# A cross-attention and expert layer: all tokens through sorted expert blocks in two phases, none through all experts

## The reference

```python
# x: (8, 256, 256); ctx: (8, 120, 256); 16 heads; 8 experts; all float32
x = x + xattn(layernorm(x), ctx, ctx, Wq, bq, Wk, bk, Wv, bv, Wo, bo, mask, key_mask)
hs = layernorm(x).reshape(-1, 256)                  # 2048 tokens
probs = softmax(hs @ router_w + router_b)           # 8 experts
idx = argmax(probs); gate = probs[idx]
expert_out = einsum('th,ehd->ted', hs, expert_w) + expert_b
x = x + (one_hot(idx) * gate) combined with expert_out   # one expert per token
```

## Time and profile before

| what | value |
|---|---|
| median of three runs | 257.46 us (257.45 to 258.82) |
| the profiled execution's own time | 259.96 us |
| its span, first to last instruction | 258.2 us |
| mean granted clock of PE | 0.921 of 2.4 GHz |
| busy: PE, DVE, ACT, POOL | 221.6, 156.4, 117.1, 74.6 us |
| chain that ended last | PE 54%, DVE 23%, ACT 6%, issue 6%, DMA 5%, POOL 4% |

### The profile page before, as it was taken

How to read it: one execution, slowest core, us unless ns; L and a number is a source line. 1 busy time by engine, 2 the same in 40 slices (tenths; PEclk the granted TensorE clock), 3 DMA queues, 4 the chain that set the end, 5 groups by cost and what they waited for, 6 DMA issues and landing times.

```text
span 258.2 us, 5042 instructions
## 1 busy us (share of the span) xinstructions
PE 221.6 (86%) x1696; PEld 153.1 (59%) x1696; DVE 156.4 (61%) x499; ACT 117.1 (45%) x254; POOL 74.6 (29%) x100
## 2 busy tenths in 40 slices
PE   7599988898988989989998995853969969999994
PEld 2376556476656666566675553532767757776683
DVE  4358763756787878779648563482433545565564
ACT  0646664665745754863763555416322340531000
POOL 6155762051144054035004004030113044124400
PEclk9979997999999999999999999995555989999799
DMA  6894005000001001000001001014121113211001
GB/s 212 305 365 137 1 1 163 7 3 1 3 0 44 1 3 41 4 0 22 23 3 41 0 3 41 4 43 116 53 62 49 55 41 94 74 50 54 20 20 41
DMA packets 12164, 14.19 MB, mean 55 GB/s; under 512 B 2257, under 2 KB 10729, under 8 KB 12138
## 3 DMA queue, kind: packets, MB, share of 16 engines
q1 hardware_dynamic: 9932, 8.79, 11.3%
q0 software_dynamic: 1488, 3.18, 3.5%
q10 hardware_dynamic: 720, 1.91, 2.2%
HBM read 9.09 MB, written 5.69 MB: 57 GB/s over the span
## 4 chain that ended last, share of the span: by engine, by line
PE 54%; DVE 23%; ACT 6%; issue 6%; DMA 5%; POOL 4%; SPq 1%; ACTq 0%; DVEq 0%; POOLq 0%
PE ps L426 11%; DVE nm L1086 10%; PE ps L414 7%; PE ps L496 5%; PE ps L492 4%; PE ps L613 4%; PE ps L420 4%; ACT pr L769 3%; DMA kp<-in_key_mask_dram 3%; PE ps L466 3%; PE ps L611 3%; PE ps L520 2%; PE ps L597 2%; PE ps L507 2%; PE ps L614 2%
## 5 line engine op out<-in xcount | busy, mean ns | idle before, releaser
L769 ACT ACTIVATE pr<-ps 120x512 f32<-120x512 f32 x64 | 33.0, 602 | 16.5 <-PE ps L496 16.5
L1086 DVE TENSOR_REDUCE nm<-ps 128x4 bf16<-128x480 f32 x64 | 37.5, 648 | 3.2 <-PE ps L470 3.2
L346 POOL DMA_INDIRECT out_dram<-e_nat,hb x19 | 18.8, 988 | 51.4 <-DVE e_nat L1133 49.4
L341 POOL DMA_INDIRECT rows_by_expert<-xr,slot x12 | 12.2, 1019 | 50.2 <-DVE slot L1055 48.3
L775 ACT ACTIVATE ou<-ps 128x512 f32<-128x512 f32 x16 | 9.6, 597 | 26.5 <-PE ps L507 24.3
L492 PE MATMUL ps<-tT,sel 128*120 128x512 bf16 x64 | 18.5, 403 | 1.8 <-ACT tT L820 1.4
L1141 DVE SCALAR_TENSOR_TENSOR xr<-ps,dsp,xr 128x256 f32<-128x256 f32 x32 | 15.5, 483 | 6.5 <-PE ps L414 5.8
L426 PE MATMUL ps<-xT,w_nat 128*128 128x256 f32 x64 | 16.6, 404 | 2.9 <-ACT xT L792 2.9
L322 POOL TENSOR_TENSOR rs<-ve,mhalf 128x2 f32<-128x2 f32 x8 | 5.6, 701 | 46.2 <-DVE ve L964 46.2
L507 PE MATMUL ps<-pr,va 120*32 120x256 f32 x256 | 17.5, 386 | 0.7 <-ACT pr L769 0.6
L597 PE MATMUL ps<-identf,hnb 128*128 128x128 f32 x38 | 9.6, 343 | 9.7 <-ACT hnb L755 7.6
(11 more groups left out here) (151 smaller groups left out, 510.4 us busy)
## 6 DMA issues: line engine op xcount, KB each, us to landing
hb<-rows_by_expert SPq DMA_DIRECT2D x19, 130.0 KB, 2.1
xr<-in_x_dram SPq DMA_DIRECT2D x8, 256.0 KB, 7.3
e_nat<-in_expert_w_dram SPq DMA_DIRECT2D x2, 1024.0 KB, 7.4
rows_by_expert<-zer SPq DMA_DIRECT2D x1, 1040.0 KB, 11.1
ctxs<-in_ctx_dram ACTq DMA_DIRECT2D x1, 840.0 KB, 6.9
out_dram<-xr SPq DMA_DIRECT2D x4, 128.0 KB, 1.7
out_dram<-e_nat,hb POOLq DMA_INDIRECT x19, 2.4
w_nat<-in_Wk_dram ACTq DMA_DIRECT2D x1, 256.0 KB, 3.4
```

The costliest lines, as they stand in the source:

```text
L346: pool.indirect_dma_start(out_rows, bass.IndirectOffsetOnAxis(ap=hb[:, j % HR, C_ID:C_ID + 1].bitcast(U32), axis=0), ob[:, j % HR, :], Non ...
L769: act.activation(pr[:, r, :, :], SC[r][0:S, :], ACT.Exp, scale=SCALE).then_inc(s("a_exp"), 1)
L1086: v.tensor_reduce(nm[:, b % 2, h, :, 2 * r:2 * r + 2], SC[r][:, 0:G * S].rearrange("p (c e s) -> p c e s", c=KC, e=2), AX_X, ALU.max, nega ...
```

## The change

All eight batches are sorted. Phase 0 holds batches 0 to 4 (10 tiles, 17 blocks), phase 1 batches 5 to 7 (6 tiles, 13 blocks), each with HBM rows, zeros, counts and a block table of its own; 30 blocks in all. `dense_unit`, its sums and its bias product are gone. The table of phase 0 is worked out at the beginning of `i` = 7, and the loads follow; the pipeline ends with `i` = 7. What was left of batches 6 and 7 is written out by hand between block steps 0 to 10; steps 11 and later are blocks alone.

The rows carry the normalised values besides the plain ones (`CW` = 514 words), so ACT no longer normalises a block, and PE transposes from the loaded buffer. The scale and offset stay in SBUF (`rs2`, `nb2`). `oner` and `ebp` have 128 rows, of which two are used and the rest are zero. PE looks up the expert's number inside the block step instead of at set places ahead. `block_low` and `block_out` are the two halves of DVE's former `block_part`.

```diff
-    SB = B - 2
-    NS = SB * TH
-    NB = NS + E - 1
+    FB = (0, 5, B)
+    NSP = [(FB[p + 1] - FB[p]) * TH for p in range(2)]
+    NBP = [n + E - 1 for n in NSP]
...
-    CW = D + 4
-    C_RS, C_NB, C_GATE, C_ID = D, D + 1, D + 2, D + 3
+    CW = 2 * D + 2
+    C_HN, C_GATE, C_ID = D, 2 * D, 2 * D + 1
...
-        ebp = sb("ebp", [33, E, D], F32R)
-        oner = sb("oner", [33, P], F32R)
+        ebp = sb("ebp", [P, E, D], F32R)
+        oner = sb("oner", [P, P], F32R)
...
-            sp.dma_start(rows_d.rearrange("(e r) d -> r e d", e=E)[0:P],
-                         zer[:, :].unsqueeze(1).to_broadcast([P, E, CW])).then_inc(s("d_z"), 16)
+            zeros = zer[:, :].unsqueeze(1).to_broadcast([P, E, CW])
+            sp.dma_start(rows_d[0].rearrange("(e r) d -> r e d", e=E)[0:P], zeros).then_inc(s("d_z0"), 16)
...
+            sp.dma_start(rows_d[1].rearrange("(e r) d -> r e d", e=E)[0:P], zeros).then_inc(s("d_z1"), 16)
...
-            sp.wait_ge(s("v_be"), 2)
-            sp.wait_ge(s("d_z"), 16)
-            sp.wait_ge(s("d_sc"), 16 * NS)
-            for j in range(NB):
-                load_block(j)
-            for t in range(NS, NT):
-                sp.wait_ge(s("v_dn"), (t // TH - SB) * NU + (EP - 1) * TH + t % TH + 1)
-                sp.dma_start(out[t // TH, (t % TH) * P:(t % TH + 1) * P, :], xr[:, t, 0:D]).then_inc(s("d_out"), 16)
+            for p in range(2):
+                sp.wait_ge(s("v_be"), 2 * p + 1)
+                sp.wait_ge(s(f"d_z{p}"), 16)
+                sp.wait_ge(s(f"d_sc{p}"), 16 * NSP[p])
+                for j in range(NBP[p]):
+                    load_block(NBP[0] * p + j)
...
-                pool.memset(oner[:, :].bitcast(F32), 1.0).then_inc(n, 1)
+                pool.memset(oner[:, :].bitcast(F32), 0.0).then_inc(n, 1)
                 pool.memset(ebp[:, :, :].bitcast(F32), 0.0).then_inc(n, 1)
-                pool.wait_ge(n, NLATE - 2)
+                pool.wait_ge(n, NLATE - 3)
+                pool.memset(oner[0:2, :].bitcast(F32), 1.0).then_inc(n, 1)
...
-                if i == B:
-                    for j in range(EARLY):
-                        store_block(j)
-                if 0 <= i - 2 < SB:
+                if 0 <= i - 2:
                     scatter(i - 2)
                 if 0 <= C < B:
                     rsqrt2(C)
-            for j in range(EARLY, NB):
+            store_block(0)
+            store_block(1)
+            rsqrt2(B - 1)
+            for j in range(2, 6):
                 store_block(j)
-
-
-
-        STEPS = {B: [[], [0], [1], [2], [3, 4], [5], [6, 7], [8]],
-                 B + 1: [[9, 10], [11], [12], [13], [14, 15], [16], [17, 18], [19, 20]]}
-        DENSE = {B: [[], [], [], [], [], [], [], [0]],
-                 B + 1: [[], [1], [2], [3], [4], [5], [6], [7]]}
-        SUMS = {B + 1: [[0], [], [1], [2], [3], [4], [5], [6]]}
-
-
-        LOADS = {B: [[], [0, 1], [2], [3, 4], [5], [6], [7, 8], [9, 10]],
-                 B + 1: [[11], [12, 13], [14], [15, 16], [17], [18], [], []]}
-
-        def at(table, i, f):
-            return table[i][f] if i in table else []
-
-        def left(table, n):
-            return range(max(sum(table[B + 1], [])) + 1, n)
+            scatter(B - 2)
+            for j in range(6, 9):
+                store_block(j)
+            scatter(B - 1)
+            for j in range(9, NB):
...
-            def load_experts(js):
-                for j in js:
-                    if j == 0:
-                        pe.wait_ge(s("v_be"), 1)
-                    if j < NB:
-                        experts[j] = pe.value_load(be[0:1, j:j + 1], min_val=0, max_val=E - 1)
 
             def block_step(j):
                 if j < NB:
-                    pe.wait_ge(s("a_hb"), j + 1)
+                    if j in (0, NBP[0]):
+                        pe.wait_ge(s("v_be"), 2 * phase_of_block(j) + 2)
+                    experts[j] = pe.value_load(be[0:1, j:j + 1], min_val=0, max_val=E - 1)
+                    pe.wait_ge(s(f"d_hb{j % HR}"), 16 * (j // HR + 1))
                     if j == 0:
                         pe.wait_ge(s("v_mx"), 2 * NP * B)
+                        pe.wait_ge(s("a_exp"), 2 * NP * B)
                     if j >= 2:
                         pe.wait_ge(s("v_bL"), j - 1)
                     for k in range(KC):
-                        t = pe.transpose(TURN[j % 2][:, k * P:(k + 1) * P], hnb[:, j % 2, k * P:(k + 1) * P], identf[:, :])
+                        t = pe.transpose(TURN[j % 2][:, k * P:(k + 1) * P],
+                                         hb[:, j % HR, C_HN + k * P:C_HN + (k + 1) * P], identf[:, :])
...
-            def dense_unit(u):
...
-                        if R == SB - 1:
-                            c_hidden_turn(R)
-                        elif isC:
...
+            c_out_turn(B - 1)
+            block_step(0)
+            block_step(1)
+            c_norm_turn(B - 1)
+            block_step(2)
+            c_project(B - 1)
+            block_step(3)
+            c_hidden_turn(B - 2)
+            block_step(4)
+            c_logits(B - 2)
+            block_step(5)
+            block_step(6)
+            pe.wait_ge(s("a_hT"), B - 1)
+            c_hidden_turn(B - 1)
+            r_ranks(B - 2)
+            block_step(7)
+            c_logits(B - 1)
+            block_step(8)
+            block_step(9)
+            block_step(10)
+            r_ranks(B - 1)
+            for j in range(11, NB + 2):
...
-                    act.activation(hnb[:, j % 2, :], hb[:, j % HR, 0:D], ACT.Identity, scale=hb[:, j % HR, C_RS:C_RS + 1],
-                                   bias=hb[:, j % HR, C_NB:C_NB + 1]).then_inc(s("a_hb"), 1)
...
+                    a = act.activation(xr[:, t, C_HN:C_HN + D], xr[:, t, 0:D], ACT.Identity, scale=rs2[:, t:t + 1],
+                                       bias=nb2[:, t:t + 1])
...
+            block_high(0)
+            block_high(1)
+            norm_high(B - 1)
+            hidden(B - 2)
+            block_high(2)
+            block_high(3)
+            hidden_high(B - 2)
+            block_high(4)
+            hidden(B - 1)
+            block_high(5)
+            gate_exp(B - 2)
+            block_high(6)
+            hidden_high(B - 1)
+            block_high(7)
+            block_high(8)
+            gate_exp(B - 1)
+            for j in range(9, NB):
+                block_high(j)
...
+            def block_step(j):
+                if j < NB:
+                    block_low(j)
+                if j >= 2:
+                    block_out(j - 2)
...
+                        if i == B - 1:
+                            blocks(0)
...
+            hidden_offset(B - 2)
+            normalise(B - 1)
+            block_step(0)
+            block_step(1)
+            block_step(2)
+            residual(B - 1)
+            block_step(3)
+            block_step(4)
+            hidden_offset(B - 1)
+            route_logits(B - 2)
+            block_step(5)
+            route_choice(B - 2)
+            block_step(6)
+            slots(B - 2)
+            block_step(7)
+            route_logits(B - 1)
+            block_step(8)
+            route_choice(B - 1)
+            block_step(9)
+            block_step(10)
+            slots(B - 1)
+            blocks(1)
+            for j in range(11, NB + 2):
+                block_step(j)
```

More of the change, by code:

```diff
@@ L194, in xattn_moe_kernel, with phase, phase_of_block, place_in_cum @@
         block = es.enter_context(nc.Block())
-        ITER = range(-1, B + 2)
-        UB = [(OV, PJ)[n % 2] for n in range(NU)] + [(OV, PJ, TR)[n % 3] for n in range(NU)]
-        def unit(u):
-            b, n = SB + u // NU, u % NU
-            return b, n // TH, n % TH, UB[u]
+        ITER = range(-1, B)
+        def phase(b):
+            return int(b >= FB[1])
+        def phase_of_block(j):
+            return int(j >= NBP[0])
+        def place_in_cum(t):
+            return t + phase(t // TH)
         TURN = [SC[0][:, 0:D], SC[1][:, 0:D]]
@@ new lines, in block_low, with block_out @@
+            def block_low(m):
+                v.wait_ge(s("a_bH"), m + 1)
+                if m >= 3:
+                    v.wait_ge(s("p_by"), m - 2)
+                v.tensor_tensor(bL[:, m % 3, :, :], TURN[m % 2].rearrange("p (k t) -> p k t", k=KC),
+                                bH[:, m % 3, :, :].bitcast(F32), ALU.subtract).then_inc(s("v_bL"), 1)
+            def block_out(m):
+                v.wait_ge(s("p_by"), m + 1)
+                if m >= HR:
+                    v.wait_ge(s(f"d_o{m % HR}"), 16 * (m // HR))
+                v.scalar_tensor_tensor(out=ob[:, m % HR, :], in0=PROD[m % 2], scalar=hb[:, m % HR, C_GATE:C_GATE + 1],
+                                       in1=hb[:, m % HR, 0:D], op0=ALU.mult, op1=ALU.add).then_inc(s("v_by"), 1)
```

300 lines of the change are left out of this document (82 added, 218 removed).

## The result

The changed kernel took 246.75 us (median of 4 runs, 243.45 to 248.84), the kernel before 257.45 beside it; the ratio is 0.950, interval 0.939 to 0.962. The direction was forecast, the size was not: 232 was said, with a range to 243, so the gain is 10.7 us where 25.5 were expected. The profiled run took 246.34, its span 244.5 at a mean granted clock of 0.944.

The account below looks back on a forecast made before the run. It took PE's tail to be bound by gaps, low clock and inefficient blocks; the new tail, laid out through 175.9, 198.5, 208.0, 212.3 and 229.7, gave span 232.3, 25.9 less, so 232 us, range 227 to 243.

Parts of the forecast that it names:

- The bias product on 128 rows: Expert block step on PE: 1.15 us at full clock instead of 1.44, about 2.0 instead of 2.52 at low clock.
- the check by parts: Whole kernel: 23 us of dense units less 13 for new blocks, 5.5 from cheaper old blocks, some 10 from gaps and clock.
- Rival (a): Block step: the gap of the bias product stays, 1.44 us a block; time 236, chance 0.08.
- Up to ranks(7): Last attention stage and block steps 2 to 10: batch 7's norm turn at 175.9 us, ranks(7) at 198.5, partly low clock.
- (c): Tail from 176 us: the clock stays low to the end, steps at 2.0; time 246, chance 0.09.
- (d): Tail: slower than before, clock low and blocks at the old low-clock price of 2.52; time 264, chance 0.03.
- the second lands 2.9 after its issue at 201.3, at 204.3: Phase change: landing of batch 7's last scatter, which leads to block 17 being there at 208.0 us.
- the ring of eight buffers, ... 10.3 for eight, 1.29: Last 13 blocks: store landing, SP, load, three steps and output take 10.3 us per eight blocks, 1.29 each.
- The 1.45: Last 13 blocks: us taken per block, expecting queueing above the competing rates; twelve intervals give 17.4.
- Rival (b): Block step limited elsewhere, by the lookup inside it or 257 KB loads taking 4.2 us; time 242, chance 0.09.
- landing 2.4 and the closing waits 0.2: Kernel end: us from the last store at 229.7 to the span's end at 232.3.
- Rival (e): Whole change: the parts cancel and little comes; chance 0.02.

Follow-up runs that it names:

- c2: The kernel before with only the bias product changed, read from 128 rows instead of 33; 248.91 us, ratio 0.966.
- e4: The changed kernel with the bias product back on 33 rows; 253.84 us, ratio 0.978 to the kernel before.
- g1: d3 with the expert lookups of all blocks put back; 235.99 us, ratio 0.912.
- g3: d3 without the constant products that hold the clock; 237.59 us, ratio 0.918.
- g5: g1 with each lookup a load alone, without the arithmetic and bounds test behind it; 235.4 us, ratio 0.910.
- d3: The changed kernel with one expert lookup, 258-word rows of plain values, twelve load buffers and constant products in PE's waits; 234.52 us, ratio 0.905.
- g2: d3 with rows of 514 words and the normalised values again; 237.23 us, ratio 0.911.
- d2: The changed kernel with the last four stores written directly by SP to a spare buffer; 240.66 us, ratio 0.932.
- c3: The changed kernel with constant, unused products in PE's waits to hold the clock; 245.26 us, ratio 0.949.
- c1: The changed kernel run again unchanged, as control; 249.41 us, ratio 0.967.
- d1: The changed kernel run again unchanged, as control for another set; 246.26 us.

## Why the prediction was right in direction and wrong in size

*The bias product on 128 rows*: right, and its gain on the low side. 1.15 was taken, 1.09 and 1.05 measured, and the part alone brought 9.7 us (c2) where the check by parts gave it 5.5 and a share of the gaps. It is followed after 0.21 and not the 0.12 said. Rival (a) is out. The Trainium skill ("TensorE: Matmul & The Clock Gate", "Why this matters for your kernels") has a product over 32 rows take what one over 128 takes. No run has 32 rows; with 33 these traces do not agree, 0.32 behind the product in e4 against 0.21 on 128 rows in the kernel after. Its other rule (same page, "LDWEIGHTS (loading the stationary operand)"), that the weight load does not depend on the rows, does agree: 0.18 and 0.19. What differs is that around the 33-row product the loads did not run ahead of their products.

*Up to ranks(7)*: right, 1.4 late at the norm turn and 1.4 at the ranks. The clock fell at 166 and again at 190, as far as "part of it low" says. One reading behind it was loose: the block work at the low level before the change was not "without a gap", PE being busy for only 1.04 us of those from 190 to 193. Two slips in the working touch only rivals (c) and (d): the 10.3 of project, turns and logits at the low clock stands on no row, and (d) decides from a step of 2.29, not 2.26.

*The phase change*: **the first step that failed, and by size the largest, is "the second lands 2.9 after its issue at 201.3, at 204.3"**. It was issued at 204.08, 2.8 late (1.4 of it since the ranks), and landed in 5.1, at 209.2. The 2.9 had been scaled from a landing with little other traffic, where here the DMA engines moved 245 GB/s (206 to 209); with half rows the same scatter landed in 2.5 in three runs of four (g1, g3, g5; 4.3 in d3). Then came a wait that the forecast did not have, 1.2 for the landing of block 9's store: the buffers of the second phase are those of the first, and I let the ring begin only behind block 17. SP and the load took 3.4 of their 3.6. Behind that, block 17's store came 6.4 after its transposes and not 4.3: 1.3 of it is the low clock of its first steps, the rest is spent at POOL, where block 16's store went 1.29 ahead of it.

*The last 13 blocks*: **the second step that failed is "the ring of eight buffers, ... 10.3 for eight, 1.29"**, worth 1.8 us here. The ring turns in six blocks, not eight, since PE does the products of block j − 2 behind the transposes of block j. With my own durations that gives 2.4 + 1.04 + 2.6 + 1.15 + 0.8 = 8.0 for six, 1.33, so most of the rest is landings: in the chain a store lands in 3.5 and a load in 2.8, and the turn took 9.8 for six, 1.63. The 1.45 was a guess over rates of 1.15 to 1.29, of which two were wrong: PE's 1.15 left out the lookup, which makes it 1.50 once PE has nothing queued. Rival (b) had the lookup, and a slow load (4.2) where slow landings in a short ring came; it gave 1.9 a block and 242 a chance of 0.09, and the divisor of six stood in no rival. With ring, lookup and clock mended POOL's rate appears, 1.29 against the forecast's 1.28, and nearly its time, 234.5 to 237.2 us (d3, g2, g5; 237.6 without the products that hold the clock, g3), though in kernels that leave a part of the computation out or change it. That the wrongly divided ring also gave 1.29 is luck.

*The end*: **the third is "landing 2.4 and the closing waits 0.2"**, which lacked 2.4. The kernel before ended with dense units and a direct store, under which POOL's drain had passed; the change puts an indirect store last, and the drain behind it. d2 shows it.

*The check by parts*, 23 less 13, failed with them: eleven more blocks cost 1.6 to 1.8 each in the place where they were put. Bias part alone 0.966, phases alone 0.978 on another chip, both 0.967 to 0.950: the phases added between nothing and 1.6 points.

Rivals (c) and (d) are out: the clock was back by 200 and steps were 1.09 where PE had work queued. The low clock did cost 4 us (c3). Rival (e) is out for the whole change, but comes close for the two phases without the bias part.

## What to carry to other kernels

Write a ring of buffers as a recurrence through the engines' program order, from the landing of one store to the issue of the next that it gates, and count the blocks between; the number of buffers is the wrong divisor when a step works on an older block. Take landings from a stretch with the traffic that the change will make. When several rates lie close together, take them off together before calling any of them innocent, and put one back at a time: together they gave 8 us here. Run the unchanged kernel beside every set of variants. And ask what comes last: an indirect transfer at the end has its queue's closing drain behind it, which the same transfer in the middle hides.

## What the runs showed of the hardware

- A product with 33 rows of weights was followed after 0.31 to 0.32 (before, e4), the same with 128 rows after 0.20 to 0.21 (c2, after), at full clock. The weight load took 0.18 and 0.19; with 33 rows it and the next one started with their products, not 0.1 ahead.
- GpSimd's closing drain ended 2.6 us after its last indirect transfer in kernels with 31 of them, 3.5 with 42, 3.8 with 46.
- Reading a value into TensorE's sequencer took 0.30, and with the arithmetic and test behind it about 0.7; without them thirty lookups did not show in stores 1.29 apart (g5).
- Indirect stores were issued at best 1.29 apart, whether they moved 128 rows or none (the last four blocks), and scatters 1.27.
- Landings were longer with more traffic: stores 2.4 before (median), 2.7 after and 3.5 to 4.8 in its chain; loads of 130 KB 2.1, of 257 KB 3.1; the last scatter 2.5 with half rows (g1, g3, g5; 4.3 in d3), 4.7 to 5.1 with full ones (g2, after).
- On one chip SP's 0.03 us instructions took up to 0.7 (c1), on another not (d1), with the same kernel; the cause is open.
